# Second graph layer: two constants read from a PSUM bank, ranks moved beside the segment products, their copy moved from ScalarE to VectorE

## What is computed

```
x = layernorm(x + L0(x, edges))            # attention; the first half of the time
gathered = vals[:, None] * x[cols]         # cols = dst, rows = src
agg = segment_sum(gathered, rows, N)
x = layernorm(x + agg @ W.T + b)
```

## Time and profile before

| | us |
|---|---|
| median of 3 runs | 10328.13 (10326.98 to 10329.69) |
| profiled execution, its own time | 10333.03 |
| its span, first to last instruction | 10331.0 |
| DVE busy over the span | 8439.9 (82%) |
| PE busy | 7745.4 (75%) |
| POOL busy | 7267.5 (70%) |
| ACT busy | 5169.5 (50%) |

### The profile page before, as it was taken

One profiled execution on the slowest core, in us unless ns is written; L12 is line 12 of the kernel. 1 busy time (PEld: TensorE's weight loads), 2 busy tenths in 40 slices (PEclk: granted clock), 3 DMA queues, 4 the chain that ended last, 5 costly groups with the idle time before them and its releaser, 6 DMA issues.

```text
span 10331.0 us, 262543 instructions
## 1 busy us (share of the span) xinstructions
PE 7745.4 (75%) x52864; PEld 7259.9 (70%) x52865; DVE 8439.9 (82%) x20927; ACT 5169.5 (50%) x21646; POOL 7267.5 (70%) x6764
## 2 busy tenths in 40 slices
PE   5577777777777777777747777877877878787845
PEld 2477777777777777777747777777877777777744
DVE  6789898999988999989885555788888888888857
ACT  1377777777777777777733333333333333333300
POOL 0577777777777777777727777777777777777710
PEclk8688888888888888888865555788788888888888
DMA  6477666666666666667612222455555455555443
GB/s 182 129 183 182 182 181 180 182 180 183 182 182 182 181 181 182 180 181 183 176 52 67 68 67 68 132 139 139 139 140 139 138 140 139 138 139 138 135 118 99
DMA packets 1646737, 1526.62 MB, mean 148 GB/s; under 512 B 796583, under 2 KB 1367619, under 8 KB 1646499
## 3 DMA queue, kind: packets, MB, share of 16 engines
q1 hardware_dynamic: 1374244, 848.34, 32.1%
q0 software_dynamic: 272384, 677.07, 23.1%
HBM read 1269.62 MB, written 254.87 MB: 148 GB/s over the span
## 4 chain that ended last, share of the span: by engine, by line
POOL 27%; issue 25%; DVE 15%; ACT 12%; DMA 7%; PE 7%; DVEq 5%; ACTq 1%; SPq 0%; POOLq 0%
POOL message_scratch L821 24%; ACT arena L1089 5%; DMA message_scratch<-ohT,idx 4%; ACT feat L1111 3%; POOL kv L789 3%; DMA kv<-kv_scratch,arena 2%; DVEq L513 2%; DVE y_all L1477 2%; PE bank L903 2%; PE bank L963 1%; DVE kve L1463 1%; DVE arena L1458 1%; ACT L1102 1%; DVE acc L1610 1%; DVE arena L1449 1%
## 5 line engine op out<-in xcount | busy, mean ns | idle before, releaser
L789 POOL DMA_INDIRECT kv<-kv_scratch,arena x3520 | 3744.5, 1064 | 1416.3 <-issue 1361.0
L821 POOL DMA_INDIRECT message_scratch<-ohT,idx x3232 | 3481.7, 1077 | 1078.2 <-issue 924.6
L1198 ACT ACTIVATE ohT<-bank,kv 128x128 f32<-128x128 f32 x3232 | 924.0, 369 | 2883.6 <-DMA message_scratch<-ohT,idx 2860.5
L1021 PE MATMUL bank<-oh,kve 128*128 128x128 f32 x8640 | 1458.0, 332 | 863.9 <-DVE arena L1770 816.1
L1021 PEld LDWEIGHTS bank<-oh,kve 128*128 128x128 f32 x8640 | 1312.8, 237 | 985.3 <-DVE arena L1770 912.1
L1089 ACT ACTIVATE arena<-arena,weights 128x65 f32<-128x65 f32 x7040 | 1771.0, 337 | 2.8 <-PE bank L930 2.8
L1011 PE MATMUL bank<-acc,oh 128*128 x6464 | 1185.5, 340 | 281.9 <-ACT ohT L1199 281.3
L930 PE MATMUL bank<-arena,oh 128*128 128x130 f32 x7040 | 1171.3, 319 | 264.9 <-DVE acc L1610 258.2
L930 PEld LDWEIGHTS bank<-arena,oh 128*128 128x128 f32 x7040 | 1056.3, 228 | 343.3 <-issue 276.1
L1011 PEld LDWEIGHTS bank<-acc,oh 128*128 128x128 f32 x6464 | 1022.6, 241 | 298.2 <-issue 298.1
L1760 DVE TENSOR_TENSOR oh<-irow,kv 128x768 f32<-128x768 f32 x720 | 690.0, 958 | 660.0 <-DVE kv L1753 535.4
(11 more groups left out here) (223 smaller groups left out, 12739.6 us busy)
## 6 DMA issues: line engine op xcount, KB each, us to landing
kve<-message_scratch SPq DMA_DIRECT2D x2160, 129.0 KB
kve<-nodes_scratch SPq DMA_DIRECT2D x880, 256.0 KB
feat<-in_edge_attr_dram SPq DMA_DIRECT2D x880, 96.0 KB
feat<-block_scratch SPq DMA_DIRECT2D x812, 98.0 KB
kv<-kv_scratch,arena POOLq DMA_INDIRECT x3520
arena<-q_scratch SPq DMA_DIRECT2D x880, 64.0 KB
message_scratch<-ohT,idx POOLq DMA_INDIRECT x3232
feat<-in_edge_attr_dram SPq DMA_DIRECT2D x880, 32.0 KB
```

Of the source, the lines that this page charges most:

```text
L789: pool.indirect_dma_start(kv[:, k, g, :], None, kv_d, bass.IndirectOffsetOnAxis(ap=took[:, j, g, 0:1].bitcast(I32), axis=0)).then_inc(s_ga ...
L821: pool.indirect_dma_start(msg_d, bass.IndirectOffsetOnAxis(ap=idx[:, k, g:g + 1], axis=0), sum_ring[:, k % RING1, g, :], None).then_inc(s_ ...
L1021: op = pe.matmul(banks[4 + sg.half][:, b * P:(b + 1) * P], mt[:, sg.slot(MT) + b, a, 0:C], seg_oh[:, sg.half, b, a, :], start=(a == 0), st ...
L1198: act.activation(sum_ring[:, st.k % RING1, g, 0:C], banks[2 + st.k % 2][:, g * P:(g + 1) * P], ACT.Copy, scale=taken[:, st.k, g, 2:3])
```

## The change

It acts on the second layer alone, in five places. (1) The ranks go to bank 4 or 5, columns 384 to 387, beside the segment products in columns 0 to 383. Banks 0 and 7 are no longer used by them. (2) Bank 7 now holds the constants: before the loop DVE copies `irow` and one column of `ones` there, and `count_stage` and `seg_onehots` read their first operand from it. (3) The copy of the ranks into the table ring moves from ACT to DVE, between `seg_add` and `place_stage`. (4) On PE the rank products move to the head of a step. As they now share a bank with the products that DVE adds, the wait for the adds (`freed_stage`) stands before them, and the segment products wait until DVE has copied the earlier ranks of that bank. (5) ACT's body loses the copy.

```diff
+        irow_ps, one_ps = banks[7][:, 0:P], banks[7][0:NB, P:P + 1]
+        RANKS = SEGMENT * P
@@ rank_stage
-                    op = pe.matmul(banks[(0, 7)[st.k % 2]][:, g:g + 1], found1[st.k % 4][0:NB, g * P:(g + 1) * P], ones[0:NB, 0:1], start=True, stop=True)
+                    op = pe.matmul(banks[4 + st.k % 2][:, RANKS + g:RANKS + g + 1], found1[st.k % 4][0:NB, g * P:(g + 1) * P], ones[0:NB, 0:1], start=True, stop=True)
@@ PE
-            def agg1_stage(sg):
+            def freed_stage(sg):
+
+                wait(pe, s_sadd, SEGMENT * (sg.n - 1))
+
+            def agg1_stage(sg, placed):
 
+                wait(pe, s_posw, placed)
                 pe.wait_ge(s_soh, sg.n + 1)
-                wait(pe, s_sadd, SEGMENT * (sg.n - 1))
@@ PE body1
+                    pair = Step1(i, k + 7)
+                    if not pairs or not exists(pair, STEPS1):
+                        placed = STEPS1 if not pairs else min(pair.before(2), STEPS1)
+                    else:
+                        placed = pair.before(2)
                     if segs:
-                        seg(i, k, 0, 1, pairs, agg1_stage)
+                        seg(i, k, 0, 1, pairs, freed_stage)
                     if pairs:
-                        at1(i, k, (row1_stage, 3), (rank_stage, 7), (sum1_stage, 1))
+                        at1(i, k, (rank_stage, 7))
+                    if segs:
+                        seg(i, k, 0, 1, pairs, lambda sg: agg1_stage(sg, placed))
+                    if pairs:
+                        at1(i, k, (row1_stage, 3), (sum1_stage, 1))
@@ ACT
-            def posw_stage(st):
-                act.wait_ge(s_rank, st.s + 1)
-                if st.k == 0:
-                    act.wait_ge(s_chunk, 16 * (st.i + 1))
-                act.activation(ring_t[:, bass.ds(ring_of(st), G), 0], banks[(0, 7)[st.k % 2]][:, 0:G], ACT.Copy).then_inc(s_posw, 1)
@@ ACT body1
-                        at1(i, k, (posw_stage, 6), (rows_out, 0))
-                    if pairs:
-                        at1(i, k, (take1, 5), (off_stage, 3))
+                        at1(i, k, (rows_out, 0), (take1, 5), (off_stage, 3))
@@ DVE
-                dve.tensor_tensor_scan(ranks[0:NB, st.k % 2, :], ones[0:NB, 0:1].to_broadcast([NB, G * P]), in_blk[0:NB, st.k % 2, :], since,
+                dve.tensor_tensor_scan(ranks[0:NB, st.k % 2, :], one_ps.to_broadcast([NB, G * P]), in_blk[0:NB, st.k % 2, :], since,
+            def posw_stage(st):
+
+                dve.wait_ge(s_rank, st.s + 1)
+                if st.k == 0:
+                    dve.wait_ge(s_chunk, 16 * (st.i + 1))
+                dve.tensor_copy(ring_t[:, bass.ds(ring_of(st), G), 0], banks[4 + st.k % 2][:, RANKS:RANKS + G]).then_inc(s_posw, 1)
-                dve.tensor_tensor(seg_oh[:, sg.half, :, :, :].rearrange("p b a n -> p (b a) n"), irow[:, :].unsqueeze(1).to_broadcast([P, 2 * SEGMENT, P]),
+                dve.tensor_tensor(seg_oh[:, sg.half, :, :, :].rearrange("p b a n -> p (b a) n"), irow_ps.unsqueeze(1).to_broadcast([P, 2 * SEGMENT, P]),
@@ DVE body1
-                        at1(i, k, (place_stage, 0), (found_stage, 8))
+                        at1(i, k, (posw_stage, 6), (place_stage, 0), (found_stage, 8))
@@ DVE, before the loop
+            dve.tensor_copy(irow_ps, irow[:, :])
+            dve.tensor_copy(one_ps, ones[0:NB, 0:1])
```

## The result

On the chip of this comparison the kernel before took 10324.81 us (median of 20 runs, 10318.94 to 10335.66) and the changed kernel 10309.39 us (20 runs, 10301.19 to 10319.49). The ratio is 0.9984, with a 95% interval from 0.9977 to 0.9990: 15 us faster. Beside the later experiments, on another chip, it was 0.9979 (0.9970 to 0.9988), 22 us. The sign was right and the size was not: -49 us was forecast, and the gain lies at the 0.2% that I had named as the least that can be told. On three other chips, met later, everything is slower, and there the same change loses 2% (measured on one of them).

The account below looks back on a forecast made before the run. POOL was taken to set the pace in the pairs alone, DVE with segments; -70 (hold gone) + 42 (copy) - 21 (tail) = -49 us gave 10284 us against the profiled execution, 10279 against the median, range 10255 to 10383.

Parts of the forecast that it names:

- The bound of the kernel: Second layer: POOL sets the pace in the pairs alone, held 0.47 us a step by the prefix sum; DVE with segments.
- Part 1: Pairs alone: the prefix sum's hold on scatters goes, gaining 0.35 us a step, 70 us (bounds 14 to 94).
- an estimate from equal phases: Pairs alone: the found product holds early-starting scatters with chance 0.44, by 0.28 us on average, 0.12 us a step.
- My bounds of 0 and 0.4: Pairs alone: bounds, in us a step, on how long the found product holds scatters, estimated at 0.12.
- Part 2: Prefix sum and segment one-hots: a bank operand adds zero to DVE's time; upper bound 0.06 us for each instruction.
- Part 3: DVE's new rank copy: free in the pairs alone, 0.07 us net on 600 segment steps, 42 us (bounds 39 to 108).
- Parts 4 and 5: PE's new order, with 1.85 us left over a step, costs zero; ACT losing 0.18 us of 5.5 gains zero.
- if PE's step no longer fitted: Condition for being wrong: PE's step, with ranks ahead of segment products, no longer fits at half clock.
- Part 6: End of the pairs: POOL catches up, its last scatter ends some 6 us behind the last place, not 27; 21 us gained.
- some four steps of the ring behind: End of the pairs, kernel before: POOL's lag behind DVE, scattering until 9849 us after the last place at 9821.8.
- the rival with 0.38: Prefix sum holds scatters despite its bank operand; only the copy's +42 us is left, 10370 us; chance 0.38.
- one row of the first layer: A gather starting 0.33 us into the bank-operand prefix sum takes 2.06 us, not 0.95, so that instruction seemed to hold.

Follow-up runs that it names:

- scan_sbuf: The changed kernel with the prefix sum's ones read from SBUF again; pairs alone went from 1078 back to 1129.5 us.
- after_third: The changed kernel, unaltered, run again beside the later experiments on another chip like the first: 0.9979 of the kernel before.
- copy_act: The changed kernel with the rank copy back on ACT and all ranks in bank 0, constants still in bank 7: 0.9925 of the kernel before, 10252 us.
- copy_dve_only: The kernel before with only the rank copy moved from ACT to DVE: 1.0047 of the kernel before.
- after_again: The changed kernel, unaltered, run again on a slow chip: 1.0201 of the kernel before.
- one_deep: The changed kernel with PE making a step's ranks after the copy one step back, not two: 1.0411 and 1.0389 of the kernel before, on slow chips.

## Why the prediction missed

- **The bound of the kernel**: right. POOL sets the pace in the pairs alone, DVE with segments, and the prefix sum was the holder (scan_sbuf).
- **Part 1, the pairs alone**: the mechanism right, the size off: 0.27 us a step and 56 us in place of 0.35 and 70. The step that failed is "an estimate from equal phases", by which a scatter starts early in the found product with chance 0.44 and is held 0.28 us. Measured from 5800 to 6400 us: 84 starts in it in 114 steps, 75 of them held, by 0.31 us on average, 0.21 us a step and not 0.12. In after_third, the other execution, it was 0.15 there. Over all 208 steps 131 scatters are held in it, for 39 us, and 125 for 35 us in after_third, where a chance of 0.44 makes 92 and 26 us. The mean scatter was 1.016 us, not 0.99. So the 0.28 us were right and the chance was not: it is 0.60 to 0.63. I read it so: DVE's step is tied to POOL's through the ring, and with the hold of the prefix sum gone, scatters drift into the next instruction that holds. No run tested this reading. A small term that I had left out: the comparison of `in_blk_stage`, with one operand in SBUF and 345 ns for 512 columns, holds too, 38 of 84 starts, 3.4 us in all. My bounds of 0 and 0.4 had the sum.
- **Part 2, bank operands cost DVE nothing**: right. The prefix sum 1274 ns against 1275, the one-hots 958 against 958. The 62 cycles that the Trainium skill, "VectorE: DVE Perf Modes", section on the TRN2 errata, gives for a read from PSUM do not show in these rows.
- **Part 3, the copy**: 0.07 us on 600 steps, 42 us; 45 measured, 54 for the copy alone. Right, and it is the largest loss of the change: copy_act is without it.
- **Parts 4 and 5, PE's order and ACT**: the order is zero here, 1.0001; that ACT has one instruction less shows no gain in copy_dve_only. On slow chips PE's order costs 1.1% alone. What I had named as a condition ("if PE's step no longer fitted") is what happened there; I had tied it to the clock alone.
- **Part 6, the tail**: POOL catches up as forecast, by step 240 to 300, and its first scatter of a step starts 0.8 to 2.3 us behind the place from there to step 790. But the gain is 11 us and not 21. The end, DVE and POOL, answers to the earlier trace rows:

```profile
9794.07 0.15 DVE L1754 TENSOR_TENSOR idx<-kv 128x4 int32<-128x4 f32 x1
...
9797.76 0.15 DVE L1754 TENSOR_TENSOR idx<-kv 128x4 int32<-128x4 f32 x1
...
9799.91 0.16 DVE L1754 TENSOR_TENSOR idx<-kv 128x4 int32<-128x4 f32 x1
...
9802.00 0.15 DVE L1754 TENSOR_TENSOR idx<-kv 128x4 int32<-128x4 f32 x1
...
9817.69 0.96 POOL L823 DMA_INDIRECT message_scratch<-ohT,idx  x1 [0.30 <-issue]
...
9827.46 0.17 DVE L1767 TENSOR_TENSOR kv<-kve,seg_base 128x6 f32<-128x6 f32 x1 [24.38 <-DMA kve<-message_scratch]
```

  The last places stand 3.7, 2.2 and 2.1 us apart, since the steps near the end have no prefix sum and no found product any more, while POOL needs 5.06 us for each. So it falls behind again, and its last scatter starts 15.5 us after the last place, not 1. The step that failed is to take the 27 us of the earlier trace rows as "some four steps of the ring behind" all along, and DVE's step as 5.61 us to the end. In the kernel before, the first scatter of a step starts 15.4 to 16.4 us behind its place from step 300 to 790, under three steps, and 22.5 us behind at the last: 7 us come up in the last eight steps. In the changed kernel some 11 us come up there, from 0.8 to 11.8 us. What the caught-up ring takes away is 22.5 - 11.8 = 10.7 us.
- **The chances**: the rival with 0.38, that the prefix sum holds all the same, rested on one row of the first layer and is refuted for the second. The traces on record answer it for the first layer too. In the kernel before, 107 of 108 gatherings that start in L1516 are held, and end 0.83 us after L1470, the instruction behind it. The one that is not held starts 0.14 us into L1516 and ends before L1470 starts. On one slow chip DVE often stands idle between the two, as in after_again (there L1523 is the prefix sum and L1477 the instruction behind it):

```profile
786.85 1.20 DVE L1523 TENSOR_TENSOR_SCAN oh<-oh,bank 16x512 f32<-16x512 f32 x1
787.19 0.95 POOL L791 DMA_INDIRECT kv<-kv_scratch,arena  x1 [0.30 <-issue]
788.42 0.49 DVE L1477 TENSOR_SCALAR ohT<-kve,arena 128x512 f32<-128x512 f32 x1 [0.36 <-issue]
```

  This gathering starts 0.34 us into the prefix sum, and the one of the earlier trace rows 0.33 us, but it takes 0.95 us and not 2.06. In the four traces from that chip 158 gatherings start in this prefix sum and have the time to end before the next instruction; 157 of them take their 0.95 us. So the prefix sum with one operand in a bank does not hold here either, and the comparison behind it does. What stays open is how that one can hold back for its full 0.83 us a gathering that is 0.8 us along.

What is left open besides: in copy_act scatters are held for 26 us in the pairs alone and in the changed kernel for 39 to 42, which covers the 10 to 12 us between them; why fewer are held there is not known. One_deep was to tell, and ran on slow chips alone.

## What to carry over

Where two engines are tied by a ring, a hold that is removed can partly be taken back by the next instruction that holds, here 35 to 39 of 94 us. Price that from the phases in the timeline, and if a bank is free, free that instruction too: the output of the prefix sum in a free bank cost DVE 13 ns each, where it waited anyway, and won 26 us. An instruction of 0.15 us on the engine that sets the pace, 0.07 us net, in 600 steps eats 45 of 67 us; the bank layout that spared it was worth 77 us (0.9925) in place of 15 to 22, on chips like the first ones. Look at the last steps of a pipeline by themselves, since they are not as long as the others. And before one held row is taken for the rule, look for a row in which the suspect stands alone.

## What had not been expected of the hardware

Chips differ: the experiments ran on five, and on three of them the same kernel took 12.67 to 12.93 ms in place of 10.33 to 10.34, with single matmuls 0.7 us apart in the trace that I looked through. A change that won 0.2% on one kind lost 2.0% on the other, and a wait that was drawn one step tighter (one_deep) lost 4%.
